# Latent attention of a nine-stage kernel: one order of single-bank score steps against one of two-bank head pairs

## What is computed

```python
def _attention(x, Wq, Wkva, Wkvb, Wo):
    q = (x @ Wq).reshape(b, t, H, D).transpose(0, 2, 1, 3)
    ckv = x @ Wkva
    kv_latent, k_rope = (ckv[:, :, :R], ckv[:, :, R:])
    kv = (kv_latent @ Wkvb).reshape(b, t, H, NOPE).transpose(0, 2, 1, 3)
    ...
    att = jnp.einsum('bhqd,bhkd->bhqk', q, k) / jnp.sqrt(jnp.float32(D))
    att = jnp.where(mask, att, jnp.float32(-jnp.inf))      # causal
    att = jax.nn.softmax(att, axis=-1)
    y = jnp.einsum('bhqk,bhkd->bqhd', att, v).reshape(b, t, H * D)
    return y @ Wo
```

## Time and profile before

| | us |
|---|---|
| runs of the kernel, three | 1953.51, 1943.57, 1965.15 |
| median | 1953.51 |
| profiled execution, span from first to last instruction | 1926.2 |
| median above that span | 27.3 |
| the latent phase in the profiled execution, its first projection to its last use of PE | 417.65 |

### The profile page before, as it was taken

One profiled execution on the slowest core, in us unless ns is written; L12 is line 12 of the kernel. 1 busy time (PEld: TensorE's weight loads), 2 busy tenths in 40 slices (PEclk: granted clock), 3 DMA queues, 4 the chain that ended last, 5 costly groups with the idle time before them and its releaser, 6 DMA issues. The chain is left out here.

```text
span 1926.2 us, 24318 instructions
## 1 busy us (share of the span) xinstructions
PE 1542.9 (80%) x9156; PEld 783.5 (41%) x9158; DVE 998.0 (52%) x1384; ACT 708.8 (37%) x1306; POOL 576.9 (30%) x602
## 2 busy tenths in 40 slices
PE   5778738899689996985579857999999857779982
PEld 3355513333334443432244334444454432245541
DVE  3799556778332326763367523333342135568855
ACT  2435224667410003762237532333332222255521
POOL 1478523543111103310024124223311110037650
PEclk7799966899889997996669868999896679979985
DMA  3000010000100001000100010000000000000000
GB/s 94 1 1 1 1 40 1 1 1 2 70 1 0 0 0 46 1 1 8 43 3 1 1 40 1 1 1 1 1 1 1 1 26 0 6 1 2 2 3 22
DMA packets 19153, 20.58 MB, mean 11 GB/s; under 512 B 9803, under 2 KB 15163, under 8 KB 18408
## 3 DMA queue, kind: packets, MB, share of 16 engines
q1 hardware_dynamic: 19048, 19.13, 3.3%
HBM read 17.94 MB, written 1.05 MB: 10 GB/s over the span
## 5 line engine op out<-in xcount | busy, mean ns | idle before, releaser
L1677 DVE TENSOR_REDUCE L2f_nm<-P 128x2 f32<-128x768 f32 (+3 forms) x88 | 99.0, 1126 | 222.4 <-PE P L1582 222.0
L1593 PE MATMUL P<-L2f_qs,L2f_ks 49*128 49x256 f32 (+3 forms) x512 | 148.2, 512 | 17.1 <-DMA L2f_qs<-L2f_mt 17.1
L1652 ACT ACTIVATE L2f_prob<-P 128x512 f32<-128x512 f32 x160 | 89.8, 597 | 188.1 <-PE P L1593 188.1
L997 DVE TENSOR_REDUCE L0f_nm<-P 128x2 f32<-128x768 f32 (+3 forms) x88 | 97.4, 1119 | 53.2 <-PE P L904 53.2
L2160 PE MATMUL P<-L0m_hm,L0m_w 128*128 128x512 f32 x256 | 112.5, 599 | 2.7 <-POOL L0m_hm L2122 2.6
L1509 POOL TENSOR_SCALAR_AFFINE_SELECT L2f_prob<-L2f_prob 128x512 f32<-128x512 f32 x64 | 39.6, 637 | 247.6 <-ACT L2f_prob L1652 247.5
L1593 PEld LDWEIGHTS P<-L2f_qs,L2f_ks 49*128 49x128 f32 x512 | 82.1, 212 | 73.1 <-issue 41.4
L1579 PE MATMUL P<-L2f_ks,L2f_qs 48*128 48x512 f32 (+3 forms) x512 | 107.7, 498 | 0.0
L953 ACT ACTIVATE L0f_prob<-P 128x512 f32<-128x512 f32 x160 | 87.1, 604 | 36.7 <-PE P L915 35.3
L2463 POOL TENSOR_TENSOR L3x_exm<-L3x_exm,L3x_rec 128x2048 f32<-128x2048 f32 x16 | 72.4, 4529 | 26.1 <-DVE L3x_rec L2637 26.1
L2160 PEld LDWEIGHTS P<-L0m_hm,L0m_w 128*128 128x128 f32 x256 | 49.1, 192 | 65.0 <-issue 62.9
(11 more groups left out here) (583 smaller groups left out, 3371.9 us busy)
## 6 DMA issues: line engine op xcount, KB each, us to landing
L0m_w<-in_L0m_w SPq DMA_DIRECT2D x1, 2048.0 KB, 7.9
L0f_va<-in_L0f_va SPq DMA_DIRECT2D x3, 512.0 KB, 4.7
in_xt<-in_x SPq DMA_DIRECT2D x1, 1024.0 KB
L0x_segi<-in_segb SPq DMA_DIRECT2D x1, 1024.0 KB, 5.0
L0m_w<-in_L0m_w SPq DMA_DIRECT2D x1, 1024.0 KB, 9.9
L2f_qs<-L2f_mt SPq DMA_DIRECT2D x64, 2.0 KB, 1.7
out<-out_o SPq DMA_DIRECT2D x4, 256.0 KB, 2.5
L1x_va<-in_va SPq DMA_DIRECT2D x3, 256.0 KB, 3.1
```

The lines of the kernel that those rows point to most:

```text
L997: nc.vector.tensor_reduce(S.nm[:, qt, first:first + 2 * many].rearrange("p (i e) -> p e i", e=2), P[:, bank:bank + 2, 0:many * width].rear ...
L1593: m = mm(P[:, bank, at:at + width], S.ks[b % 2][64 * e:64 * e + 49, kt * 128:(kt + 1) * 128], S.qs[b % 2][64 * e:64 * e + 49, pair, q0:q0 ...
L1652: nc.scalar.activation(S.group_prob(b, g)[:, slot, :], P[:, bank, :], ACT.Exp).then_inc(*S.act_done.up())
L1677: nc.vector.tensor_reduce(S.nm[:, qt, first:first + 2 * many].rearrange("p (i e) -> p e i", e=2), P[:, bank:bank + 2, 0:many * width].rear ...
```

## The change

The class `LatentHeads` is replaced by `LatentPairs`, with a new order. All of PE's score work is in head pairs:

- One exponential step (`uA0`, `vB1` and so on in the string) now does both heads of a pair, e = 0 and 1 in alternation, into two neighbouring banks, and one ScalarE instruction takes the exponential of both (128x1024). There are 10 to a half in place of 20. A group of four heads is now two pairs.
- `p` and `t1` fill two banks too, and are evicted with one ScalarE instruction; `k` does its two products in one step.
- These and the rounds share one ring of three slots of two banks each (banks 0 to 5); `lat`, `t2` and `out` share the single bank 7; the values stay in bank 6. A round has to wait for the use three before it, whatever that was.
- The mask matmuls are gone. VectorE adds the mask to the diagonal blocks in PSUM, in place, and reduces after that.
- The maxima go to `qs` in two DMAs of four rows in place of eight of one.
- `vc` goes through the key tiles in its outer loop. Functions that nothing calls are deleted, and the values' weights are laid out for the new groups.

```diff
-    RING = ("k", "lat", "p", "t1", "t2", "A", "B", "C", "out")
-    BY_DVE = ("k", "out")
+    DOUBLE = ("k", "p", "t1", "round", "A", "B", "C")
+    SINGLE = ("lat", "t2", "out")
+    BY_DVE = ("k", "round", "out")
+    SLOTS = 3
...
+    def slot_for(self, pe, step):
+
+        n = self.place[step]
+        if n > self.SLOTS:
+            pe.wait_ge(*self.gone(self.double[n - 1 - self.SLOTS]))
+        return 2 * ((n - 1) % self.SLOTS)
...
+STEP_latent_order = """w R0 la R1 lb lc t0 R2 lt uA0 R3 uA1 sa ka uB0 R4 uB1 sb kl p0 uC R5 sc rec vA0 ma R6 vA1 sd turn mb vB0 x0 R7 mc mt
+ vB1 se t1 R8 p1 x1 vC R9 sf out res R10""".split()
...
-                    for h in range(8):
-                        row = 64 * (h % 2) + 48
-                        sp.dma_start(S.qs[b % 2][row:row + 1, 4 * half + h // 2, :], S.mt[half][h:h + 1, :])\
+                    for e in range(2):
+                        sp.dma_start(S.qs[b % 2][64 * e + 48:64 * e + 49, 4 * half:4 * half + 4, :], S.mt[half][e:8:2, :])\
                             .then_inc(*S.rows_ready.up(16))
...
                 elif kind == "t2":
-                    pe.wait_ge(S.s_free.sem, max(S.place[r] for r in S.place if r[0] == "round" and r[1] == b and r[2][0] == n))
-                    bank = S.ring_use(pe, s)
+                    pe.wait_ge(S.dve_done.sem, S.rounds_of(b, n))
+                    bank = S.bank_for(pe, s)
...
-                            mm(P[:, bank + e, p * width:(p + 1) * width], S.qs[b % 2][64 * e:64 * e + 48, pair, qt * 128:(qt + 1) * 128],
-                               S.ks[b % 2][64 * e:64 * e + 48, 0:width], start=p == 0, stop=False)
-                    for e in range(2):
-                        m = mm(P[:, bank + e, 0:many * width].rearrange("p (h k) -> p h k", k=width)[:, :, width - 128:width],
-                               G["identb"][:], mask[:].unsqueeze(1).to_broadcast([128, many, 128]), start=False, stop=True)
-                    m.then_inc(*S.s_full.up())
+                            m = mm(P[:, bank + e, p * width:(p + 1) * width], S.qs[b % 2][64 * e:64 * e + 48, pair, qt * 128:(qt + 1) * 128],
+                                   S.ks[b % 2][64 * e:64 * e + 48, 0:width], start=True, stop=True)
+                    m.then_inc(*S.full.up())
                 elif kind in S.EXPS:
...
+                    bank = S.slot_for(pe, s)
+                    tiles = ([(2 * g + i, 0, 0, 0, T)] if kind == "A" else
+                             [(2 * g + i, 1, 0, 128, 384), (2 * g + i, 3, 384, 384, 128)] if kind == "B" else
+                             [(2 * g + x, 2, 256 * x, 256, 256) for x in range(2)])
+                    for pair, kt, at, q0, width in tiles:
+                        for e in range(2):
+                            m = mm(P[:, bank + e, at:at + width], S.ks[b % 2][64 * e:64 * e + 49, kt * 128:(kt + 1) * 128],
+                                   S.qs[b % 2][64 * e:64 * e + 49, pair, q0:q0 + width], start=True, stop=True)
+                    m.then_inc(*S.full.up())
...
-                    nc.scalar.activation(S.group_prob(b, g)[:, slot, :], P[:, bank, :], ACT.Exp).then_inc(*S.act_done.up())
+                    at = {"A": 2 * i, "B": 4 + 2 * i, "C": 8}[kind]
+                    nc.scalar.activation(S.prob_of(b, g)[:, at:at + 2, :], P[:, bank:bank + 2, :], ACT.Exp).then_inc(*S.act_done.up())
...
+                    at = P[:, bank:bank + 2, 0:many * width].rearrange("p e (i k) -> p e i k", k=width)
+                    diag = at[:, :, :, width - 128:width]
+                    link(dve, nc.vector.tensor_tensor(diag, diag, mask[:].unsqueeze(1).unsqueeze(1).to_broadcast([128, 2, many, 128]),
+                                                      ALU.add), S.vstep)
                     first = 8 * half + 2 * many * i
-                    nc.vector.tensor_reduce(S.nm[:, qt, first:first + 2 * many].rearrange("p (i e) -> p e i", e=2),
-                                            P[:, bank:bank + 2, 0:many * width].rearrange("p e (i k) -> p e i k", k=width),
-                                            AX.X, ALU.max, negate=True).then_inc(*S.s_free.up())
+                    nc.vector.tensor_reduce(S.nm[:, qt, first:first + 2 * many].rearrange("p (i e) -> p e i", e=2), at,
+                                            AX.X, ALU.max, negate=True).then_inc(*S.dve_done.up())
```

More of the change, by code:

```diff
@@ new lines, in gone, with slot_of, bank_for @@
+    def gone(self, step):
+        return (self.dve_done if step[0] in self.BY_DVE else self.act_done).sem, self.freed[step]
+    def slot_for(self, pe, step):
[3 more added lines that the diff above has]
+        return 2 * ((n - 1) % self.SLOTS)
+    def slot_of(self, eng, step):
+        eng.wait_ge(self.full.sem, self.place[step])
+        return 2 * ((self.place[step] - 1) % self.SLOTS)
+    def bank_for(self, pe, step):
+        n = self.place[step]
+        if n > 1:
+            pe.wait_ge(*self.gone(self.single[n - 2]))
+        return 7
@@ new lines, in bank_of, with rounds_of, units_of, prob_of @@
+    def bank_of(self, eng, step):
+        eng.wait_ge(self.one_full.sem, self.place[step])
+        return 7
+    def rounds_of(self, b, half):
+        return max(self.freed[r] for r in self.freed if r[0] == "round" and r[1] == b and r[2][0] == half)
+    def units_of(self, b, g, part):
+        return max(self.freed[part, b, (g, i)] for i in range(1 if part == "C" else 2))
+    def prob_of(self, b, g):
+        return self.prob[(4 * b + g) % 3]
+STEP_latent_order = """w R0 la R1 lb lc t0 R2 lt uA0 R3 uA1 sa ka uB0 R4 uB1 sb kl p0 uC R5 sc rec vA0 ma R6 vA1 sd turn mb vB0 x0 R7 mc mt
+ vB1 se t1 R8 p1 x1 vC R9 sf out res R10""".split()
@@ L1433, in one @@
             return (name, b - 1, 0) if half == 0 and b else None
+        if name == "w":
+            return ("t2", b, half)
         if name[0] == "t":
[L1435 to L1446, removed]
+            return ("t1", b + 1, 2 * half + n) if b + 1 < NB else None
+        if name in ("ka", "kl"):
+            return ("lat" if name == "kl" else "k", b + 1, 0) if half == 0 and b + 1 < NB else None
+        return (name[0], b + 2, 2 * half + n) if b + 2 < NB else None
+    project = lambda b: [s for qt in range(QT) for s in (("p", b, qt), ("x", b, qt))]
+    order = [("k", 0, 0), ("lat", 0, 0)] + project(0) + [("t1", 0, 0), ("t1", 0, 1)]
+    order += spread_between(project(1) + [("t1", 0, 2), ("t1", 0, 3)], rounds(0))
     for h in range(2 * NB):
@@ L1469, in phase_latent_heads, with shape_of @@
     norm((ld, loads), sq=S.prob[0][:, 0:NB, :])
-    heads = lambda half, e: [8 * half + 2 * j + e for j in range(4)]
+    def shape_of(step):
+        half, qt, i = step[2]
+        return half, qt, i, (4, 2, 1, 1)[qt], 128 * (qt + 1)
     with nc.Block() as block:
@@ L1501, in _ @@
                 elif kind == "sel":
[L1502 to L1505, removed]
+                    g, part = n
+                    pr = S.prob_of(b, g)
+                    pool.wait_ge(S.act_done.sem, S.units_of(b, g, part))
                     diag = {"A": [pr[:, 0:4, 0:128]], "B": [pr[:, 4:8, 0:128], pr[:, 4:8, 384:512]],
@@ L1565, in _ @@
                 elif kind == "round":
-                    half, qt, i = n
-                    if S.first["round", b, half] == s:
-                        pe.wait_ge(S.act_done.sem, max(S.freed["t1", b, 4 * half + x] for x in range(4)))
+                    half, qt, i, many, width = shape_of(s)
+                    if S.leads["round", b, half] == s:
+                        pe.wait_ge(S.act_done.sem, max(S.freed["t1", b, 2 * half], S.freed["t1", b, 2 * half + 1]))
                         pe.wait_ge(S.k_ready.sem, b + 1)
-                    use = S.place[s]
@@ L1602, in _ @@
                             pe.wait_ge(S.o_free.sem, 4 * b + n)
[L1603 to L1609 removed]
+                    pe.wait_ge(S.sel_ready.sem, S.place["sel", b, (n, kind[1].upper())])
+                    pr = S.prob_of(b, n)
+                    for kt, at, q0, width in {"va": [(0, 0, 0, T)], "vb": [(1, 0, 128, 384)], "vc": [(2, 0, 256, 256), (3, 384, 384, 128)]}[kind]:
+                        for j in range(4):
+                            slot, col = (8 + j % 2, 256 * (j // 2)) if kt == 2 else (j if kt == 0 else 4 + j, at)
+                            m = mm(P[32 * j:32 * j + 32, 6, q0:q0 + width], S.va[b % 3][:, kt, :], pr[:, slot, col:col + width],
                                    start=kt == 0, stop=kt == 3)
@@ L1687, in _ @@
                     if b:
[L1688 removed]
+                        dve.wait_ge(S.one_full.sem, S.place["out", b - 1, 0])
                     for gp in range(2):
```

523 lines of the change are left out of this document (99 added, 424 removed).

## The result

| | before | after |
|---|---|---|
| median of the runs, us | 1949.09 (four runs, 1943.57 to 1965.15) | 1831.30 (four runs, 1830.85 to 1833.02) |
| span of the profiled execution, us | 1926.2 | 1829.6 |
| mean granted clock over that span | 0.849 | 0.861 |
| from the first turn of maxima to the phase's last use of PE, us | 368.0 | 268.9 |
| of it at 1.2 GHz (a fall is one unbroken stretch of it) | 95.6 in six falls, longest 58.0 | 23.8 in seven falls of 3.4 |

The ratio of after to before is 0.943 (95% interval 0.940 to 0.947). The forecast was faster, but 1894 us; the range ended at 1856, 25 us above what came.

The account below looks back on a forecast made before the run. PE was taken as the bound. Seven steady halves gain 42 us, the last 9; 320 us at full clock become 269, with low clock 309, 59 less than 368. 1926.2 - 59 = 1867, with 27.3 about 1894; range 1856 to 1936.

Parts of the forecast that it names:

- the additions: VectorE's mask additions in PSUM: 0.42, 0.68 and 1.20 us by width, 5.9 us per half, hidden as a sum.
- The new wait at the turn: PE idles before each turn of the maxima until VectorE finishes the last round: 2.1 us mean over seven halves.
- the slots: Ring slots come free only when a round is reduced; behind wide rounds this costs PE 0.6 us per half.
- the rival in which the additions are dear: VectorE decides: additions cost double, each half loses about 2 us, 14 in seven: 1908 us; chance 0.12.
- The 27.3 us added to the span: Difference between the earlier kernel's median and profiled span, added to the predicted span of 1867 to give about 1894 us.
- How much of them falls to 1.2 GHz I take as before, 26%: Low-clock share of the stretch after the start-up, kept at 96 of 368: 269 us at full clock become 309.
- A steady half's gain of 6: Net gain per steady half, 4.3 + 2.8 + 1.7 - 2.1 - 0.6 = 5.9, called 6; seven make 42 us.
- the pairs: Exponential steps on PE, ten pairs of 1.06 us per half: gain 4.3 us per half, bounds 3.8 and 5.5.
- the masks: Mask matmuls taken off PE, 22 records per half: gain taken as 2.8 us per half.
- The rival with the clock up: Nothing runs at 1.2 GHz after the start-up, so 309 us become 269: 1854 us; chance 0.15.
- The clock going down: Waits at each turn and behind slots put 75% of the time at 1.2 GHz: 62 slower, 2016 us; chance 0.10.
- That pairs don't overlap: Four heads in a row take some 3.6 us, 18 per half, eating the masks' gain: 1957 us; chance 0.06.

Follow-up runs that it names:

- serial_exp: The changed kernel, but both heads of an exponential pair are computed from the even head's operands on the same partitions; 1933.35 us.
- serial_wait: The kernel wait_pairs, but both heads of an exponential pair are computed from the even head's operands, one after the other; 1977.81 us.
- wait_pairs: The changed kernel, but with eight DMAs for the rows of maxima and each half's first pair placed earlier, so PE waits before it; 1849.35 us.
- serial_rounds: The changed kernel, but the rounds of scores for the maxima use the even heads' partitions for both heads, exponentials still in pairs; 1954.26 us.
- serial_both: The changed kernel, but rounds and exponentials both run by single heads on the same partitions; 2156.87 us.
- Theory R: Expectation tested by serial_rounds and serial_both: a fall lasts until a run of steps without a single head has passed; 1954.26 and 2156.87 us.
- the twenty later runs: The kernel before, unchanged, timed beside the experiments; 1917.77 to 1978.05 us.
- cover_turn: The changed kernel, but two products with values of the group before stand ahead of the turn of the maxima; 1815.33 us.
- cover3: The changed kernel, but next-half rounds stand ahead of each turn through the whole order, and pairs are moved away from wide rounds; 1809.49 us.

## Why the prediction was wrong

**What held.** The steps as the prediction put them, with what came: the additions 428, 696 and 1233 ns (0.42, 0.68 and 1.20); a pair 1.06 us from start to start, as here from 1271.34 to the next step:

```profile
1271.34 1.13 PE L1614 MATMUL P<-L2f_qs,L2f_ks 49*128 49x512 f32 x4 [0.64 <-DVE L2f_nm L1697]
1272.40 1.13 PE L1561 MATMUL P<-Z,L2f_wka 128*128 128x512 f32 x2
```

The new wait at the turn was 17.7 in eight, 2.2 each (2.1); the slots cost 4.7 + 1.7 us, 0.8 per half (0.6); the wait for the DMA was 0 (0). ScalarE's exponential of two banks took 1025 ns (1012 for a copy of that size), and no wait of PE names it; the 1.11 us in the prediction's comparison stands in no row. The last half with the tail gained 8.7 us of work (9). So the rival in which the additions are dear fell as well.

**The 27.3 us added to the span: wrong, 26 us of the miss.** They were taken as what lies around a span, because the profiled execution had no time of its own in the list. It is 1.7 us in every run here that lists both. The median of a kernel whose runs spread by 60 us says nothing of what surrounds the span of one of them.

**"How much of them falls to 1.2 GHz I take as before, 26%": wrong, 28 us.** The forecast lost 40 us to the low clock (309 less 269); 11.9 were lost, 9% of the stretch being low. The reason given, "because a wait of like size remains in each half", was true (17.7 us for 17.1) and did not carry: the length of a fall hangs on what PE runs in it. Nor do waits alone start falls. In the kernels with both steps in pairs every fall stands behind a stretch with idle PE, as in the one shown; but both 37.5 us falls of serial_exp began behind 3.3 us and more in which PE was busy throughout. Single heads make some falls long, pairs keep them short; serial_exp against after, serial_wait against wait_pairs and serial_rounds against after show it, each pair with one order of the work. The profile of before held the hint: in the earlier trace rows PE was busy for all of 58.1 us at 0.50, so a lack of busy time, as the profile counts it, could not be what kept the clock down. The prediction mentioned that a pair keeps both halves of the rows busy, but only as a point against a rival, and priced it nowhere.

**A steady half's gain of 6: too small, 12 us.** By length times clock the seven gained 54 in place of 42. In the half of the earlier trace rows the pairs gained 5.2 (4.3 was taken, 5.5 was the bound), the masks 3.7 (2.8), the rounds 0.6, or 1.5 by the next half, which has no fall (nothing). I had chosen prices from start to start inside one run of steps, where the busy time of the whole half was the better measure.

26, 28 and 12, less 2.3 by which the rest of the program was longer, make the miss of 63. The rival with the clock up, 1827 in span, came out near the 1829.6 by two errors that cancel: it had 12 us too much work and no low clock, and 12 were lost to it.

**The rivals.** The clock going down was the wrong sign. The page TensorE: Matmul & The Clock Gate of the Trainium skill (A second HAM failure mode: psum-queue depth-cycling) was cited for it; small idles with cycling banks are there in after, and the clock did fall seven times, but for 3.4 us each. The same page of the Trainium skill (What's actually happening) has idling bring the half clock and busy time lift it; serial_exp's 37.5 us at 0.50 with PE busy for 37.50 does not fit that, and the measurement decides. That pairs don't overlap fell with the start-to-start of 1.06; its price was fair, as serial_exp's 316 against before's 320 shows.

**What stays open.** What ends a fall was read from a few places and tested only by changing which steps are single heads; serial_both's size was not foreseen. Theory R is not the exact condition either: in serial_exp 3.8 us without a single head, from 1410.36 on, did not end the fall shown, and in serial_wait 2.9 us of projections, from 1379.15 on, did end one. Whether the rows in use or something that goes with them counts was not told apart. Of the 118 us between the medians, 97 are between the two profiled spans; the other 21 lie between before's profiled execution and its median run. That they are low clock is argued from the twenty later runs, where longer times go with lower clocks; those four runs have no clock listed, and their phase was not seen. The new order, the ring and the wider evictions were not undone by themselves: 257 us with the pairs' 59 and the masks' 13 make 329, 9 above before, so they may have cost some, if these figures add up.

## What to carry to other kernels

Take the span and the time from the same execution, and where runs of one kernel spread, look at the granted clock before anything else. When PE runs matmuls that use half of its rows, put them in pairs on both halves: besides the overlap, falls of the clock here then ended after 3.4 to 6.8 us ahead of the phase's tail, where single heads left some of 13.6 to 61.4. A wait that a change introduces at a hand-over can often be covered by moving work of the next block ahead of it; here that was worth another 16 us in cover_turn and 22 in cover3.

## What was not expected of the hardware

- A busy share of 100%, which counts any matmul, does not keep the clock at 2.4 GHz. With single heads it stayed at 1.2 for up to 61.4 us, and in serial_exp it fell out of a stretch in which PE was busy for 3.30 of 3.30 us. In the changed kernel no fall from the first turn on lasted over 3.4 us.
- The kernel before spread from 1917.77 to 1978.05 us with clocks of 0.860 to 0.826, the changed one from 1830.85 to 1833.02 with 0.860 to 0.862. The two profiles of the kernel before differ in where the falls lie and how long they are; whether that makes the whole spread was not seen.
- An addition on VectorE that reads PSUM and writes it in place costs about what a product that only reads it does: 428 ns for 128x256, beside 416 before.
